# A four-layer graph network on one core: a third output bank in the last layer, one bank for transposed h, and a new order on every engine

## The chip, the core and the metric

The kernel runs on one core of a Trainium2 chip. The core has five engines with a queue of instructions each, which wait for one another by semaphores: TensorE (PE in the profile; its weight loads are PEld) multiplies matrices and writes to PSUM, VectorE (DVE), ScalarE (ACT) and GpSimd (POOL) work element by element, and SyncE (SP) issues the transfers. PSUM has 8 banks of 512 float32 numbers in each of 128 partitions. The metric is the device time of one launch in microseconds. The median before the change was 299.49 us.

## The reference

32 independent graphs of 256 nodes with 128 features pass through four residual layers. Each begins with a layer norm and a ReLU:

```python
def _layernorm(x, axis=-1, eps=1e-05):
    m = jnp.mean(x, axis=axis, keepdims=True)
    v = jnp.var(x, axis=axis, keepdims=True)
    return (x - m) / jnp.sqrt(v + eps)
h = jnp.maximum(_layernorm(x, axis=-1), 0.0)
x = x + _L0_gnn_ref(h, adj, L0_gnn_W, L0_gnn_a)
h = jnp.maximum(_layernorm(x, axis=-1), 0.0)
x = x + _L1_gnn_ref(h, adj, L1_gnn_a0, L1_gnn_a1, L1_gnn_a2, L1_gnn_a3)
h = jnp.maximum(_layernorm(x, axis=-1), 0.0)
x = x + _L2_gnn_ref(h, L2_gnn_adj, adj, L2_gnn_weight, L2_gnn_bias)
h = jnp.maximum(_layernorm(x, axis=-1), 0.0)
x = x + _L3_gnn_ref(h, adj, L3_gnn_W, L3_gnn_a)
```

Layers 0 and 3 are graph attention: Wh = h W, scores s1 of the row plus s2 of the column with W h and the vector a, leaky ReLU, softmax over the edges, times Wh. Layer 3 has an ELU behind that. Layer 1 scores an edge by the product of h of its two nodes, weighted by a vector for the relation, and averages h itself. Layer 2 sums h over the edges of each relation and multiplies by the relation's matrix.

## The kernel before

A unit is one layer of one graph: n counts 128 of them. The order (ORDER) is layer 0 of graphs 0 to 15, layer 1 of the same, layer 2, layer 3, and then the same for graphs 16 to 31. So units 0 to 15 and 64 to 79 are layer 0, 16 to 31 layer 1, 32 to 47 layer 2, 48 to 63 layer 3, and 112 to 127 layer 3 of the second half.

Every engine runs its own `pipeline` over a table of entries (stage, lag, layers). In step s it goes through the table from top to bottom and issues the stage for unit s - lag, if that unit's layer is meant. So a lag sets in which step a stage comes, and the place in the table its order within the step. At a border between layers a step holds stages of both. The tables are written out by hand; nothing is reordered later.

The way of a unit of layer 0 or 3: VectorE takes statistics (`statistics`, L574), aggregates them to mean and variance (`mean_and_variance`, L582) and adds eps (`add_eps`, L588). GpSimd raises to the power -0.5 (`inverse_deviation`, L346), subtracts the mean (L354) and scales (L360). TensorE transposes h (`put_hT`, L823) and ScalarE copies it with a ReLU to hT (`take_hT`, L447). TensorE multiplies by the weights (`put_v`, L851). ScalarE takes exponentials of the scores (L471) and scales the values (L479). TensorE transposes the row scores (`put_z`, L888), VectorE combines them with the edges (`take_rows`, L644, writes pT), and TensorE makes the output (`put_o`, L926 and L929). VectorE inverts the sums (L654, L656). In layer 0 it then adds the residual (L670). In layer 3 ScalarE takes the ELU's two parts (`elu_parts`, L516 and L517, written expy and relu_y), and VectorE adds them (`elu`, L678) and adds x (`add_x`, L687, writes result). In layer 0 ScalarE also masks the edges (L456), TensorE transposes them (`put_edgesT`, L838) and ScalarE copies them (L466). In layer 1 VectorE rectifies h (`rectify`, L593); in layer 2 it multiplies minus the mean by the deviation (`minus_mean`, L598), and ScalarE normalizes (L437).

Banks before: transposed h uses bank 0 in layer 0, where bank 1 holds the transposed edges, and banks 0 and 1 in turn in layers 1 and 3. Outputs use banks 6 and 7 in turn, so an output waits until the one two units earlier has been taken. The weights of layers 0 and 3 (w_gat, a_gat) are both loaded on ScalarE's queue and prepared in banks 6 and 7 ahead of the first unit.

## Time and profile before

| | us |
|---|---|
| three runs | 299.09, 299.49, 300.00 |
| the profiled execution | 299.55 |
| its span | 297.7 |
| TensorE busy | 279.9 (94%) |
| VectorE busy | 261.3 (88%) |
| ScalarE busy | 260.2 (87%) |
| GpSimd busy | 224.8 (76%) |

The span is what the records of the profile cover; the execution's own time is 1.85 us longer. Busy shares are averages over four layers that load the engines differently, and matmuls overlap, so that a busy TensorE may still be slower than its own pace. So the distance between the starts of one recurring instruction says more. Idle time in brackets is that of the engine before the row, with what ended it.

### The profile page before, as it was taken

How to read it: one execution, taken by the hardware profiler on the slowest of the kernel's cores; microseconds unless marked ns; L12 is line 12 of the kernel's file. 1: busy time of each engine (PE TensorE's matmuls, PEld its weight loads, DVE VectorE, ACT ScalarE, POOL GpSimd, SP SyncE). 2: the span in 40 equal slices, each digit the busy share in tenths (PEclk: the TensorE clock that was granted, in tenths of full speed). 3: DMA queues.
4: the chain of work that ended last, by engine and by line, in shares of the span. 5: the costliest groups of instructions: out<-in, count | busy, mean ns of one | idle time of the engine just before them, and what ended most of it. 6: DMA issues, size and time to landing. Idle time of an engine off the chain costs nothing.

```text
span 297.7 us, 8186 instructions
## 1 busy us (share of the span) xinstructions
PE 279.9 (94%) x2250; PEld 259.4 (87%) x2250; DVE 261.3 (88%) x1355; ACT 260.2 (87%) x849; POOL 224.8 (76%) x363
## 2 busy tenths in 40 slices
PE   1899999999998999999999999999999899999992
PEld 1799998888987999998888999998888799999991
DVE  2689999888888898999999999988888889799995
ACT  3799997799999985899999889799999998589993
POOL 4987777676776999987768787777677699997800
PEclk9999999999999999999999999999999999999997
DMA  6925555310000000011111660000000000001223
GB/s 185 356 72 160 166 166 148 116 47 0 2 1 2 0 3 1 3 36 55 53 57 53 191 204 1 3 1 2 0 3 0 3 1 0 2 3 36 74 72 107
DMA packets 15949, 17.77 MB, mean 60 GB/s; under 512 B 2720, under 2 KB 11808, under 8 KB 15904
## 3 DMA queue, kind: packets, MB, share of 16 engines
q1 hardware_dynamic: 15072, 17.11, 18.2%
q8 instruction: 19, 0.31, 0.5%
q10 hardware_dynamic: 832, 0.13, 0.3%
q14 instruction: 26, 0.21, 0.3%
HBM read 13.05 MB, written 4.19 MB: 58 GB/s over the span
## 4 chain that ended last, share of the span: by engine, by line
PE 67%; DVE 20%; ACT 6%; issue 3%; DMA 1%; ACTq 0%; DVEq 0%
PE bank L929 19%; PE bank L875 9%; PE bank L880 9%; DVE pT L644 6%; PE bank L851 6%; PE bank L823 5%; PE bank L914 5%; PE bank L900 4%; DVE result L687 4%; DVE st L574 3%; PE bank L926 3%; PE bank L888 2%; PE bank L882 2%; PE bank L838 2%; DVE expy L678 2%
## 5 line engine op out<-in xcount | busy, mean ns | idle before, releaser
L346 POOL TENSOR_TENSOR rs<-ve,minus_half 128x2 f32<-128x2 f32 x128 | 89.9, 702 | 53.7 <-DVE ve L588 51.9
L929 PE MATMUL bank<-val,pT 128*128 128x129 f32 x512 | 74.7, 275 | 0.0
L929 PEld LDWEIGHTS bank<-val,pT 128*128 128x128 f32 x512 | 67.9, 193 | 0.0
L360 POOL TENSOR_TENSOR h<-h,rs 128x256 f32<-128x256 f32 x96 | 59.8, 623 | 0.1
L644 DVE SCALAR_TENSOR_TENSOR pT<-bank,val,edgesT 128x256 f32<-128x256 f32 x128 | 55.8, 478 | 3.7 <-PE bank L888 3.4
L574 DVE BATCH_NORM_STATS2 st<-x 128x6 f32<-128x128 f32 x192 | 44.3, 272 | 0.0
L851 PE MATMUL bank<-w_gat,hT 128*128 128x131 f32 x256 | 42.2, 288 | 0.3 <-ACT hT L447 0.2
L354 POOL TENSOR_TENSOR h<-x,mv 128x256 f32<-128x256 f32 x64 | 39.9, 623 | 2.5
L479 ACT ACTIVATE val<-bank,val 128x128 f32<-128x128 f32 x128 | 41.3, 391 | 0.0
L926 PE MATMUL bank<-ident,vsum 128*128 128x128 f32 x128 | 35.5, 278 | 3.3 <-DVE x L670 1.0
L823 PE MATMUL bank<-ident,h 128*128 128x128 f32 x192 | 38.5, 283 | 0.0
L880 PE MATMUL bank<-hT,haT 128*128 128x256 f32 x128 | 37.5, 388 | 0.1
L625 DVE CUSTOM_DVE_ANT_0 neg_s<-bank,upper 128x256 f32<-128x256 f32 x64 | 24.7, 422 | 13.3 <-ACT upper L497 13.1
L929 PEld LDWEIGHTS bank<-h,pT 128*128 128x128 f32 x256 | 31.1, 191 | 5.8 <-issue 2.0
L851 PEld LDWEIGHTS bank<-w_gat,hT 128*128 128x128 f32 x256 | 34.5, 195 | 1.5 <-issue 1.1
L929 PE MATMUL bank<-h,pT 128*128 128x129 f32 x256 | 34.1, 276 | 1.6 <-ACT pT L509 1.6
L875 PE MATMUL bank<-edgesT,h 128*128 128x256 f32 x128 | 32.6, 380 | 0.0
L582 DVE BATCH_NORM_AGGREGATE mv<-st 128x2 f32<-128x6 f32 x256 | 30.4, 160 | 0.4
L447 ACT ACTIVATE hT<-bank 128x256 f32<-128x256 f32 x64 | 26.2, 409 | 4.6 <-PE bank L823 4.2
L502 ACT ACTIVATE prob<-neg_s,neg_max 128x256 f32<-128x256 f32 x64 | 28.7, 497 | 0.0
L437 ACT ACTIVATE h<-x,nb,rs 128x128 f32<-128x128 f32 x64 | 27.8, 483 | 0.0
L588 DVE TENSOR_SCALAR ve<-mv 128x2 f32<-128x2 f32 x128 | 27.4, 214 | 0.0
(80 smaller groups left out, 664.8 us busy)
## 6 DMA issues: line engine op xcount, KB each, us to landing
edges<-in_adj SPq DMA_DIRECT2D x32, 256.0 KB, 3.5
xin<-in_x SPq DMA_DIRECT2D x32, 128.0 KB, 2.7
out_x<-result SPq DMA_DIRECT2D x32, 128.0 KB, 1.7
w_rel<-in_L_gnn_weight SPq DMA_DIRECT2D x1, 256.0 KB, 3.5
w_gat<-in_L_gnn_W ACTq DMA_DIRECT2D x2, 64.0 KB, 3.4
a_rel<-in_L_gnn_a SPq DMA_DIRECT2D x4, 0.5 KB, 4.3
bias<-in_L_gnn_bias SPq DMA_DIRECT2D x1, 64.0 KB, 3.6
a_gat<-in_L_gnn_a ACTq DMA_DIRECT2D x2, 1.0 KB, 3.5
```

The lines of the kernel that those rows point to most:

```text
L346: pool.tensor_tensor(rs[:, g % WIDE], ve[:, g % WIDE], minus_half[:, :], ALU.pow).then_inc(rs_ready, 1)
L354: pool.tensor_tensor(h[:, n % HS, :, 0:D], xin[:, g % XS] if layer == 0 else x1[:, g % WIDE], mv[:, g % WIDE, :, 0:1].to_broadcast([P, T, ...
L360: pool.tensor_tensor(h[:, n % HS, :, 0:D], h[:, n % HS, :, 0:D], rs[:, g % WIDE, :].rearrange("p (t o) -> p t o", o=1).to_broadcast([P, T, ...
L479: last = act.activation(val[:, k, t, 0:D], bank_v(n)[:, t, 0:D], ACT.Copy, scale=val[:, k, t, D:D + 1])
L574: last = dve.bn_stats(st[:, g % WIDE, t], src[:, t])
L644: last = dve.scalar_tensor_tensor(pT[:, n % 4, u], bank_z(n)[:, 0], val[:, k, u, D + 2:D + 3], edgesT[:, g % WIDE, u], ALU.max, ALU.mult)
L823: last = pe.transpose(bank_x(n)[:, t * P:(t + 1) * P], h[:, n % HS, t, 0:D], ident[:, :])
L851: last = pe.matmul(bank_v(n)[:, t], hT[:, n % 4, t * P:(t + 1) * P], w_gat[layer // 3][:, 0:D + 3], start=True, stop=True)
L875: last = pe.matmul(z[:, 0], h[:, n % HS, u, 0:D], edgesT[:, g % WIDE, u], start=(u == 0), stop=(u == T - 1))
L880: pe.matmul(z[:, t], haT[:, n % 4, t * P:(t + 1) * P], hT[:, n % 4], start=True, stop=False, skip_group_check=True)
L926: pe.matmul(bank_o(n)[:, t, 0:D], vsum[:, k:k + 1].to_broadcast([P, P]), ident[:, :], start=True, stop=False, is_transpose=True, skip_grou ...
L929: last = pe.matmul(bank_o(n)[:, t], pT[:, n % 4, u, t * P:(t + 1) * P], values[:, u], start=(u == 0 and layer == 1), stop=(u == T - 1), sk ...
```

## The change

Six things are changed.

- Outputs have a third bank, bank 1, in layer 3, from unit 48 to 57 and from 112 to 127 (the least recently used of three); from unit 58 to 63 and in the other layers they have two. Where a third bank is in use an output waits for the one three units earlier. The transposed edges, which need bank 1 in layer 0, wait for the last such output.
- Transposed h has bank 0 alone. So `put_hT` of a unit waits for `take_hT` of the unit before.
- Eps comes into the variance by the aggregation: the statistics have three more numbers a row, (0, 0, D * EPS), written once, and `bn_aggr` reads nine numbers in place of six. `add_eps` and its tile ve are gone; the power on GpSimd takes the variance from mv.
- The last layer's weights are loaded by SyncE behind x of graph 2 and prepared in units 4, 6 and 7 of layer 0, in columns of bank 0 that transposed h leaves free.
- `elu_parts` waits for `add_x` of four units before, which is the tile that it overwrites.
- All tables of lags are new, in lags and in order.

The lags that matter here, before and after: TensorE v 4 to 5, edges 4 to 5, z 5 to 6 (layer 1: 4 to 5), pT 6 to 7, o 7 to 8, transposed h stays at 3. ScalarE `take_hT` 5 to 4, `mask_edges` 4 to 5, `take_edgesT` 5 to 6, `elu_parts` 9 to 10, `scale_hT` 6 to 4, `exponentials` 7 to 6, `take_mh` 8 to 6, `normalize` 5 to 4. VectorE `take_rows` 8 to 9, `invert_sums` 10 to 11, `elu` 12 to 13, `add_x` 14 to 13, `rectify` 5 to 4, `minus_mean` 5 to 3. GpSimd 8 and 9 to 14, 15 and 16 throughout, with the power now last in a step. SyncE 8 to 11.

```diff
-LAG_MAX = 14
-SP_LAG = 8
+LAG_MAX = 16
+SP_LAG = 11
-def banks_of_hT():
...
-HT_BANK, HT_AFTER, EDGEST_AFTER = banks_of_hT()
+def banks_of_o():
+    least_used, last, bank, after = [6, 7, 1], {}, {}, {}
+    for n, (layer, _) in enumerate(ORDER):
+        third = layer == 3 and (n + 6 >= len(ORDER) or ORDER[n + 6][0] == 3)
+        bank[n] = next(b for b in least_used if b != 1 or third)
+        after[n] = last.get(bank[n])
+        last[bank[n]] = n
+        least_used.remove(bank[n])
+        least_used.append(bank[n])
+    return bank, after
+O_BANK, O_AFTER = banks_of_o()
+THIRD = [n for n in range(len(ORDER)) if O_BANK[n] == 1]
-        st = sb("st", [P, WIDE, T, 6])
+        st = sb("st", [P, WIDE, T, 9])
-        ve = sb("ve", [P, WIDE, T])
         def bank_x(n):
-            return bank[HT_BANK[n]][:, 0:N]
+            return bank[0][:, 0:N]
         def bank_o(n):
-            return bank[6 + n % 2][:, 0:T * (1 + D)].rearrange("p (t c) -> p t c", t=T)
+            return bank[O_BANK[n]][:, 0:T * (1 + D)].rearrange("p (t c) -> p t c", t=T)
...
@@ sync: loads of the first units
+                if k == 2:
+                    sp.dma_start(w_gat[1][:, 0:D], w3).then_inc(gat_loaded[1], 16)
+                    sp.dma_start(a_gat[1][:, :], a3.rearrange("(c p) o -> p (c o)", c=2), allow_slow_non_contiguous=True).then_inc(gat_loaded[1], 16)
@@ gpsimd
-            pool.wait_ge(ident_ready, 7)
+            pool.memset(st[:, :, :, 6:8], 0.0).then_inc(ident_ready, 1)
+            pool.memset(st[:, :, :, 8:9], D * EPS).then_inc(ident_ready, 1)
+            pool.wait_ge(ident_ready, 9)
-                pool.wait_ge(ve_ready, nth(ALL, n))
-                pool.tensor_tensor(rs[:, g % WIDE], ve[:, g % WIDE], minus_half[:, :], ALU.pow).then_inc(rs_ready, 1)
+                pool.wait_ge(mv_ready, nth(ALL, n))
+                pool.tensor_tensor(rs[:, g % WIDE], mv[:, g % WIDE, :, 1], minus_half[:, :], ALU.pow).then_inc(rs_ready, 1)
...
@@ scalar, take_hT: the last layer's weights in units 4, 6 and 7
+                if ORDER[n] == (0, 4):
+                    scale_a(1)
+                    take_wT(1, bank[0])
+                if ORDER[n] == (0, 6):
+                    take_wa(1, bank[0])
+                if ORDER[n] == (0, 7):
+                    act.wait_ge(norms_put, 1)
+                    act.activation(norm_sums[:, :], bank[0][0:1, 500:504], ACT.Copy).then_inc(norms_taken, 1)
@@ scalar, elu_parts
                 act.wait_ge(rinv_ready, nth(ATTEND, n))
+                if nth(LAST, n) > 4:
+                    act.wait_ge(result_ready, nth(LAST, n) - 4)
@@ vector
-                    last = dve.bn_stats(st[:, g % WIDE, t], src[:, t])
+                    last = dve.bn_stats(st[:, g % WIDE, t, 0:6], src[:, t])
...
-            def add_eps(n, layer, g):
-                k = g % SLOTS
-                dve.wait_ge(mv_ready, nth(ALL, n))
-                dve.tensor_scalar(ve[:, g % WIDE], mv[:, g % WIDE, :, 1], EPS, None, ALU.add).then_inc(ve_ready, 1)
@@ vector, its table of lags: two of the entries
-                      (residual, 11, RGCN_REL), (take_rows, 8, LAST), (rectify, 5, MULTI_REL),
+                      (take_rows, 9, LAST), (mean_and_variance, 2, FIRST), (rectify, 4, MULTI_REL),
@@ tensor, put_hT
-                if HT_AFTER[n]:
...
+                if n > 0:
+                    pe.wait_ge(hT_ready, nth(ATTEND, n) - 1)
...
+                if ORDER[n] == (0, 4):
+                    put_wT(1, bank[0])
+                if ORDER[n] == (0, 6):
+                    put_wa(1, bank[0])
+                if ORDER[n] == (0, 7):
+                    pe.wait_ge(norms_ready, 2)
+                    pe.matmul(bank[0][0:1, 500:504], ones[:, :], norms[:, :], start=True,
+                              stop=True).then_inc(norms_put, 1)
@@ tensor, put_edgesT
+                if nth(FIRST, n) > 1:
+                    pe.wait_ge(edgesT_ready, nth(FIRST, n) - 1)
+                before = [m for m in THIRD if m < n]
+                if before and g % WIDE == 0:
+                    pe.wait_ge(y_ready, nth(LAST, before[-1]))
@@ tensor, put_o
-                if n >= 2:
-                    if ORDER[n - 2][0] == 3:
-                        pe.wait_ge(y_ready, nth(LAST, n - 2))
+                before = O_AFTER[n]
+                if before is not None:
+                    if ORDER[before][0] == 3:
+                        pe.wait_ge(y_ready, nth(LAST, before))
                     else:
-                        pe.wait_ge(o_taken, nth(NOT_LAST, n - 2))
+                        pe.wait_ge(o_taken, nth(NOT_LAST, before))
+                if n in THIRD:
+                    pe.wait_ge(edgesT_ready, nth(FIRST, n))
```

On TensorE, the start of the program before (ident,w_gat and a_four,w_gatT are the weights' preparation, ident,h transposed h, ident_bf,absent the edges, w_gat,hT v, ident,val the row transposes z):

```order
L800 MATMUL bank<-ident,w_gat 128x128 x2
L804 MATMUL bank<-a_four,w_gatT 128x4 x2
L808 MATMUL bank<-norms,ones 1x4
L823 MATMUL bank<-ident,h 128x128 x2
L838 MATMUL bank<-ident_bf,absent 128x128 x4
L851 MATMUL bank<-w_gat,hT 128x131 x2
L823 MATMUL bank<-ident,h 128x128 x2
L888 MATMUL bank<-ident,val 128x128 x2
L838 MATMUL bank<-ident_bf,absent 128x128 x4
L851 MATMUL bank<-w_gat,hT 128x131 x2
L854 MATMUL bank<-hsum,w_gat 128x2
L823 MATMUL bank<-ident,h 128x128 x2
```

and now:

```order
L816 MATMUL bank<-ident,w_gat 128x128
L821 MATMUL bank<-a_four,w_gatT 128x4
L835 MATMUL bank<-ident,h 128x128 x4
L877 MATMUL bank<-w_gat,hT 128x131 x2
L861 MATMUL bank<-ident_bf,absent 128x128 x4
L835 MATMUL bank<-ident,h 128x128 x2
L914 MATMUL bank<-ident,val 128x128 x2
L877 MATMUL bank<-w_gat,hT 128x131 x2
L880 MATMUL bank<-hsum,w_gat 128x2
L861 MATMUL bank<-ident_bf,absent 128x128 x4
L835 MATMUL bank<-ident,h 128x128 x2
L914 MATMUL bank<-ident,val 128x128 x2
```

The weights of the last layer and their norms are gone from the front, two units' h are transposed ahead of the first v, and each v stands one unit further behind its h.

On VectorE, one step of the overlap of layer 3 with the next half's layer 0, before:

```order
L582 BN_AGGR mv<-st 128x2 x2
L574 BN_STATS st<-xin 128x6 x2
L644 SCALAR_TENSOR_TENSOR pT<-bank,val,edgesT 128x256 x2
L687 SCALAR_TENSOR_TENSOR result<-expy,x 128x256
L654 TENSOR_SCALAR sums<-bank 128x2
L656 RECIPROCAL rinv<-sums 128x2
L588 TENSOR_SCALAR ve<-mv 128x2
L678 SCALAR_TENSOR_TENSOR expy<-expy,relu_y 128x256
```

and now:

```order
L606 BN_AGGR mv<-st 128x2 x2
L595 BN_STATS st<-xin 128x6 x2
L705 SCALAR_TENSOR_TENSOR result<-expy,x 128x256
L696 SCALAR_TENSOR_TENSOR expy<-expy,relu_y 128x256
L672 TENSOR_SCALAR sums<-bank 128x2
L674 RECIPROCAL rinv<-sums 128x2
L662 SCALAR_TENSOR_TENSOR pT<-bank,val,edgesT 128x256 x2
```

The eps addition is gone, and add_x (result) and the ELU sum (expy) stand next to each other behind the statistics, where add_x stood behind the rows (pT) before.

On VectorE in layer 2, before:

```order
L664 TENSOR_TENSOR x<-bank,xb 128x256
L588 TENSOR_SCALAR ve<-mv 128x2
L598 SCALAR_TENSOR_TENSOR nb<-mv,rs 128x2
L582 BN_AGGR mv<-st 128x2 x2
L574 BN_STATS st<-x 128x6 x2
```

and now:

```order
L682 TENSOR_TENSOR x<-bank,xb 128x256
L595 BN_STATS st<-x 128x6 x2
L606 BN_AGGR mv<-st 128x2 x2
L617 SCALAR_TENSOR_TENSOR nb<-mv,rs 128x2
L682 TENSOR_TENSOR x<-bank,xb 128x256
```

The product with minus the mean (nb) belongs to the unit just before that of the aggregation ahead of it, where it was three units before.

## Rows read from the trace of the kernel before

**Rows 1.** Busy time in stretches: length, then PE, PEld, DVE, ACT, POOL busy

```profile
48.00:92.00 44.00, 42.87 (x318) 37.34 (x316) 37.04 (x224) 40.93 (x95) 31.28 (x49) 1.00 0.14 40
92.00:114.00 22.00, 21.47 (x135) 19.72 (x136) 20.09 (x120) 18.38 (x48) 19.64 (x30) 1.00 0.01 2
137.00:171.00 34.00, 31.74 (x284) 29.30 (x283) 33.55 (x152) 32.46 (x126) 25.63 (x40) 1.00 0.27 85
188.00:233.00 45.00, 44.75 (x338) 39.49 (x336) 38.23 (x227) 42.83 (x102) 32.81 (x52) 1.00 0.01 2
233.00:255.00 22.00, 21.44 (x135) 19.69 (x136) 20.01 (x120) 18.41 (x48) 19.71 (x30) 1.00 0.01 2
```

**Rows 2.** Timeline of the first microseconds: start, duration, engine, line, operation [idle before]

```profile
6.73 0.15 DVE L588 TENSOR_SCALAR ve<-mv 128x2 f32<-128x2 f32 x1
6.96 0.70 POOL L346 TENSOR_TENSOR rs<-ve,minus_half 128x2 f32<-128x2 f32 x1 [0.91 <-DVE ve L588]
8.64 0.69 PE L823 MATMUL bank<-ident,h 128*128 128x128 f32 x2
8.76 0.69 POOL L346 TENSOR_TENSOR rs<-ve,minus_half 128x2 f32<-128x2 f32 x1
...
12.31 1.18 PE L851 MATMUL bank<-w_gat,hT 128*128 128x131 f32 x4
15.64 0.27 PE L926 MATMUL bank<-ident,vsum 128*128 128x128 f32 x1
16.75 0.38 PE L888 MATMUL bank<-ident,val 128*128 128x128 f32 x2
17.19 0.67 PE L851 MATMUL bank<-w_gat,hT 128*128 128x131 f32 x4
```

**Rows 3.** Timeline of TensorE: row transposes (L888) of units 15, 52, 58 and 71

```profile
47.51 0.38 PE L888 MATMUL bank<-ident,val 128*128 128x128 f32 x2
...
124.51 0.38 PE L888 MATMUL bank<-ident,val 128*128 128x128 f32 x2
...
137.10 0.38 PE L888 MATMUL bank<-ident,val 128*128 128x128 f32 x2
...
170.91 0.38 PE L888 MATMUL bank<-ident,val 128*128 128x128 f32 x2
```

**Rows 4.** Chain of waits, 140 to 150 us: start, length, piece

```profile
142.30 0.78 DVE pT L644 x2
...
143.93 0.15 DVE ve L588
...
144.93 0.78 DVE pT L644 x2
```

**Rows 5.** Timeline of VectorE and GpSimd around 129 and 143 us

```profile
129.26 0.41 DVE L687 SCALAR_TENSOR_TENSOR result<-expy,x 128x256 f32<-128x256 f32 x1
...
129.82 0.69 POOL L346 TENSOR_TENSOR rs<-ve,minus_half 128x2 f32<-128x2 f32 x1 [0.53 <-DVE ve L588]
129.92 0.40 DVE L678 SCALAR_TENSOR_TENSOR expy<-expy,relu_y 128x256 f32<-128x256 f32 x1
...
142.85 0.61 POOL L354 TENSOR_TENSOR h<-xin,mv 128x256 f32<-128x256 f32 x1
142.99 0.76 DVE L687 SCALAR_TENSOR_TENSOR result<-expy,x 128x256 f32<-128x256 f32 x1
```

**Rows 6.** Timeline of ScalarE: first ELU activation of two units in a row

```profile
152.30 0.42 ACT L516 ACTIVATE expy<-bank,rinv 128x128 f32<-128x128 f32 x1
...
155.30 0.51 ACT L516 ACTIVATE expy<-bank,rinv 128x128 f32<-128x128 f32 x1
```

**Rows 7.** Page, groups of instructions: the aggregation, count, busy, mean ns | idle before

```profile
L582 DVE BATCH_NORM_AGGREGATE mv<-st 128x2 f32<-128x6 f32 x256 | 30.4, 160 | 0.4
```

**Rows 8.** Timeline of the tail

```profile
290.78 0.37 ACT L516 ACTIVATE expy<-bank,rinv 128x128 f32<-128x128 f32 x1 [0.43 <-DVE rinv L656]
...
292.16 0.37 ACT L516 ACTIVATE expy<-bank,rinv 128x128 f32<-128x128 f32 x1 [0.23 <-DVE rinv L656]
```

More of the change, by code:

```diff
@@ L423, in _, with take_wT, take_wa @@
                 act.activation(a_four[i][:, 3:4], a_gat[i][:, 1:2], ACT.Copy, scale=SLOPE).then_inc(a_scaled, 1)
+            def take_wT(i, b):
                 act.wait_ge(wT_done, i + 1)
-                act.activation(w_gatT[i][:, :], ps_w[i][:, 0:D], ACT.Copy).then_inc(wT_ready, 1)
-            for i in range(2):
+                act.activation(w_gatT[i][:, :], b[:, 256:256 + D], ACT.Copy).then_inc(wT_ready, 1)
+            def take_wa(i, b):
                 act.wait_ge(wa_done, i + 1)
-                act.activation(w_gat[i][:, D:D + 4], ps_w[i][:, 256:260], ACT.Copy).then_inc(constants, 1)
-            for i in range(2):
-                last = act.activation(norms[:, 2 * i:2 * i + 2], ps_w[i][:, 256:258], ACT.Square)
-            last.then_inc(norms_ready, 1)
+                act.activation(w_gat[i][:, D:D + 4], b[:, 500:504], ACT.Copy).then_inc(constants, 1)
+                act.activation(norms[:, 2 * i:2 * i + 2], b[:, 500:502], ACT.Square).then_inc(norms_ready, 1)
+            scale_a(0)
+            take_wT(0, ps_w)
+            take_wa(0, ps_w)
             def normalize(n, layer, g):
@@ L795, in turn, with put_wT, put_wa @@
                 pe.wait_ge(g_step, g * G + AT[name])
[L797 to L798 removed]
+            pe.wait_ge(ident_ready, 9)
+            def put_wT(i, b):
                 pe.wait_ge(gat_loaded[i], GAT_WEIGHTS)
[L800 to L801 removed]
+                pe.transpose(b[:, 256:256 + D], w_gat[i][:, 0:D], ident[:, :]).then_inc(wT_done, 1)
+            def put_wa(i, b):
                 pe.wait_ge(wT_ready, i + 1)
                 pe.wait_ge(a_scaled, i + 1)
[L804 to L808 removed]
+                pe.matmul(b[:, 500:504], w_gatT[i][:, :], a_four[i][:, :], start=True, stop=True).then_inc(wa_done, 1)
+            put_wT(0, ps_w)
+            put_wa(0, ps_w)
             def put_hT(n, layer, g):
                 k = g % SLOTS
[L812 to L817 removed]
+                if n > 0:
+                    pe.wait_ge(hT_ready, nth(ATTEND, n) - 1)
                 if layer == 1:
```

99 lines of the change are left out of this document (35 added, 64 removed).

## The prediction

> **What bounds the kernel now.** I read the busy table by stretches first, then the starts of one recurring TensorE instruction, then the chain of waits where those starts spread out, and last the timeline around each spread.
>
> The stretches [rows 1] show TensorE (PE) nearly always busy, so the question is only where its steady pace is broken. It idles 1.13 us in 48 to 92 (layer 1), 0.53 in 92 to 114 (layer 2), and 0.25 and 0.56 in the second half's counterparts: 2.5 us together. In 137 to 171, where the last layer of the first sixteen units overlaps the first layer of the next sixteen, it idles 2.26, and there VectorE (DVE) is busy 33.55 of 34 us and ScalarE 32.46.
>
> Busy time hides stretched work, so I take the row transposes of line 888, one pair for each unit of layers 0 and 3 [rows 3]. Unit 2 comes at 16.75 [rows 2] and unit 15 at 47.51: 2.37 us a unit in layer 0, TensorE's own pace. Units 52 to 58 take 12.59, 2.10 a unit in the last layer, again its own pace. Units 58 to 71 take 33.81. At the two own paces, five units at 2.10 and eight at 2.37, they would take 29.4. So 4.4 us are lost there, the largest loss of the kernel.
>
> The chain of waits says on whom: between 142.30 and 144.93 it lies wholly on VectorE, 2.63 us for one unit [rows 4], of which 0.15 is the addition of eps (ve). From 152.30 to 155.30 ScalarE needs 3.00 us for a unit [rows 6], because a unit there carries ELU parts and also masking and edge copies. So first VectorE bounds, then ScalarE.
>
> **The change part by part.** The profiled execution took 299.55 us, a span of 297.7 and 1.85 around it; that is 0.06 above the median of 299.49, so a sum against the one serves for the other.
>
> *Start.* GpSimd (POOL) waits 0.91 us for unit 1's eps addition [rows 2], which stands behind the statistics of unit 2, which wait for a load. Now the power takes the variance directly and stands behind no later unit. With the 0.15 of the addition itself and a handover, GpSimd's chain starts about 1.2 us sooner, and the first transposes of h move from 8.64 to about 7.4; the last layer's weights no longer stand ahead of them either. From there GpSimd gives a unit each 1.80 (6.96 to 8.76). The new order needs h of unit 4 in place of unit 3 before the first full step: 7.4 + 4 x 1.80 = 14.6, then one output (15.64 to 16.75, 1.1 us), and unit 2's row transposes would come at 15.7. But the weight matmuls at 12.31 take 1.18 us against 0.67 for the same four at 17.19: by that spacing TensorE ran at the lower of its two levels (1.2 GHz) there, though the records grant it 1.00, and it had been little busy before. A sparser start keeps that cost, some 0.4. So 16.1 against 16.75, and one h transpose more is done (0.2), against 0.3 for the last layer's weight matmuls that now stand inside busy steps. Term: -0.5. Bounds: -1.3 if the level rises as soon as before, +0.5 if it rises two microseconds later. The two loads moved to SP's queue stand in front of x of unit 3 and later; those are needed 1.8 us apart and the bytes ahead of them are the same, so nothing.
>
> *VectorE in the overlap.* One unit loses the 0.15 of the eps addition. The last addition shows 0.41 at 129.26 and 0.76 at 142.99, where GpSimd's subtraction (142.85, 0.61) runs beside it [rows 5]. In the new order it stands right behind the statistics, when GpSimd has just been given its power; an ELU sum of the same shape is not stretched beside a power (129.92, 0.40, beside 129.82, 0.69). So the 0.35 should mostly go too: 2.63 - 0.15 - 0.35 = 2.13, next to TensorE's 2.10. What is then late is ScalarE: four units at 3.00 against 2.37 are 2.5 us, which no reordering removes. I take a loss of 2.5 in place of 4.4: -1.9. Bounds: -4.4 (all of it, if the longer pipeline covers ScalarE's burst) and +1.0 (the additions still collide and the ELU sum as well, and TensorE waits on ScalarE's ELU with less slack, since there the outputs have two banks again).
>
> The Trainium skill ("SBUF — State Buffer", Who interferes with whom) says that a VectorE instruction with two SBUF inputs is blocked by any GpSimd instruction that reads SBUF. The rows at 142.85 agree, those at 129.82 do not: the power reads SBUF as well and the ELU sum kept its 0.40. By that rule the addition would be blocked in the new place too, up to 0.70 a unit, and this gain would be lost; that is the first rival's case.
>
> *Borders of the layers.* Every consumer now stands one step further behind its producer (hT to v two steps, z two before o), so a late ScalarE or VectorE step reaches TensorE less often. Of the 2.5 us of idle time I take 0.7: the same work still has to pass ScalarE, 40.93 of 44 busy in layer 1. Term -0.7, bounds -2.5 and +0.5.
>
> *One bank for transposed h.* A transpose now waits for the copy of the unit before. Between them lies all the rest of a unit's work on TensorE, 2.10 us less the transposes, and the copy is one ScalarE instruction. Cost 0; if ScalarE is a whole step late it costs what ScalarE is late, which is in the bounds above.
>
> *Third output bank.* It lets an output start before the ELU parts of two units earlier are done. In the tail ScalarE waits 0.43 and 0.23 for the sums of the last two outputs [rows 8], which themselves waited for ScalarE to free a bank. With those outputs earlier, ScalarE runs through: 0.66. The last additions are also queued one step less behind (13 in place of 14), 0.25. Term -0.9, bounds -1.5 and +1.0 (two units' ELU parts, eight instructions of at most 0.37 us, are left later than before, partly beside TensorE).
>
> *Longer aggregation.* Nine numbers in place of six in 256 instructions of 160 ns [rows 7]. No row shows the longer form; it costs nothing, or half as much again, 80 ns twice a unit over some twelve bound units, 1.9. I take 0: the eps addition of two numbers took 0.15 too, so the time is hardly that of the numbers.
>
> Sum: -0.5 - 1.9 - 0.7 - 0.9 = -4.0. So 299.55 - 4.0, about 295.5 us.
>
> **The rivals.**
>
> First: the overlap stays as it is but for the 0.15. The additions collide with GpSimd at their new place, so VectorE keeps about 2.5 a unit over the seven to eight units it bounds: 1.1 in place of 1.9. ScalarE's bursts fall on outputs with two banks, so the border gain is nothing, and the start is a wash. For it: the same stretch shows both collision and none. Then -1.1 - 0.9 = -2.0: 297.5 us.
>
> Second, slower: VectorE and GpSimd in a tight circle. Rectifying (layer 1) moves from lag 5 to 4 and the product with minus the mean (layer 2) from 5 to 3, one VectorE step behind the aggregation whose power they need. The circle in layer 1 is a power (0.70), a scaling (0.61), a rectifying and two aggregations (some 0.6 by [rows 7]) and handovers (0.08 each by 6.73 + 0.15 against 6.96, four of them), 2.2 us; layer 1 gives a unit 44/16 = 2.75 [rows 1]. It decides once GpSimd is still at another 0.61 when the aggregation lands: 2.8. A collision of 0.35 on top makes 3.15, 0.4 a unit over 16 of the 32 units: +6.5, and 295.5 + 6.5 = 302 us. Against it: GpSimd is busy only 31.28 of 44 there. In layer 2 it is busier (19.64 of 22), but its power and bias addition, 0.70 and about as much, still fit in 22/16 = 1.38.
>
> Third: the longer pipeline hides ScalarE's burst also, and the borders' idle time halves: -4.4 - 1.2 - 0.5 - 0.9 = -7.0, 292.5 us.
>
> **How the numbers follow.** Forecast 295.5, chance 0.56. First rival 297.5, 0.24. Second 302, 0.13. Third 292.5, 0.07. The range is 292.9 to 299.8: it holds the forecast's own spread and the first rival's, and leaves out most of the second and third. A measurement tells 0.3% (0.9 us) from no change, so faster means under 298.6. All of the third, nearly all of the forecast's and three quarters of the first rival's chance lie there: 0.78. Within 0.3%: 0.09. Slower: 0.13.
>
> **What would show it.** First transposes of h near 7.4 us and unit 2's row transposes near 16.1. In the overlap the last addition at 0.41 and VectorE's unit near 2.15; ScalarE the one that is waited for, near 3.0 a unit. Units 58 to 71 in about 32. In the tail no ScalarE wait for inverted sums. If layer 1 takes over 2.75 a unit, with VectorE waiting for GpSimd at the rectifying, the second rival is right; if the last addition still shows 0.76, the first. The forecast is wrong if the overlap is not shorter by more than 1 us, or if any layer's own pace has changed.

## The result, and the profile after

Measured in the same session, the kernel before takes 299.43 us (299.09 to 300.0, four runs) and the kernel after 294.75 us (294.44 to 295.32, four runs): a ratio of 0.9844, interval 0.9822 to 0.9866. The profiled execution's span went from 297.7 to 292.9 us, 4.8 less. The forecast of 295.5 was 0.75 too high, within its range, and the direction was right. The sum was right for partly wrong reasons, though, and the stretches show it.

Where the prediction used line 888, line 914 does the same work now: the row transposes of a unit of layers 0 and 3. The timeline of TensorE in the kernel after, units 2, 14, 48, 58, 71, 78, 112 and 127 (start, duration, engine, line, operation):

```profile
15.80 0.38 PE L914 MATMUL bank<-ident,val 128*128 128x128 f32 x2
...
43.87 0.38 PE L914 MATMUL bank<-ident,val 128*128 128x128 f32 x2
...
112.85 0.38 PE L914 MATMUL bank<-ident,val 128*128 128x128 f32 x2
...
134.69 0.38 PE L914 MATMUL bank<-ident,val 128*128 128x128 f32 x2
...
167.27 0.38 PE L914 MATMUL bank<-ident,val 128*128 128x128 f32 x2
...
183.28 0.38 PE L914 MATMUL bank<-ident,val 128*128 128x128 f32 x2
...
251.44 0.38 PE L914 MATMUL bank<-ident,val 128*128 128x128 f32 x2
...
284.35 0.38 PE L914 MATMUL bank<-ident,val 128*128 128x128 f32 x2
```

The kernel before has units 2, 58 and 71 in [rows 2] and [rows 3]; these are its units 14, 48, 78, 112 and 127:

```profile
45.11 0.38 PE L888 MATMUL bank<-ident,val 128*128 128x128 f32 x2
...
116.38 0.38 PE L888 MATMUL bank<-ident,val 128*128 128x128 f32 x2
...
187.36 0.38 PE L888 MATMUL bank<-ident,val 128*128 128x128 f32 x2
...
257.41 0.38 PE L888 MATMUL bank<-ident,val 128*128 128x128 f32 x2
...
288.47 0.38 PE L888 MATMUL bank<-ident,val 128*128 128x128 f32 x2
```

The differences of these starts divide the 4.8 us. A border is the change from one layer to the next.

| stretch | what runs there | before | after | change |
|---|---|---|---|---|
| 0 to unit 2 | start | 16.75 | 15.80 | -0.95 |
| 2 to 14 | layer 0 | 28.36 | 28.07 | -0.29 |
| 14 to 48 | border, layer 1, border, layer 2 | 71.27 | 68.98 | -2.29 |
| 48 to 58 | layer 3 alone | 20.72 | 21.84 | +1.12 |
| 58 to 71 | layer 3 beside the next layer 0 | 33.81 | 32.58 | -1.23 |
| 71 to 78 | layer 0 | 16.45 | 16.01 | -0.44 |
| 78 to 112 | border, layer 1, border, layer 2 | 70.05 | 68.16 | -1.89 |
| 112 to 127 | layer 3 alone | 31.06 | 32.91 | +1.85 |
| 127 to the end | tail | 9.23 | 8.55 | -0.68 |

So the stretches with layers 1 and 2 gave most (-4.2), and the steps in which layer 3 runs alone lost 3.0, which the forecast doesn't have.

*The start.* Its timeline, GpSimd and TensorE:

```profile
5.63 0.69 POOL L351 TENSOR_TENSOR rs<-mv,minus_half 128x2 f32<-128x2 f32 x1
...
6.96 0.69 PE L835 MATMUL bank<-ident,h 128*128 128x128 f32 x2 [1.54 <-POOL h L365]
...
9.29 1.08 PE L877 MATMUL bank<-w_gat,hT 128*128 128x131 f32 x4
...
13.60 0.61 PE L877 MATMUL bank<-w_gat,hT 128*128 128x131 f32 x4
```

Unit 1's power (5.63) has no wait in brackets now, where [rows 2] had 0.91, and the first transposes of h come at 6.96 in place of 8.64. The weight matmuls still take 1.08 at 9.29 and only 0.61 at 13.60: the slow spacing at the start stayed, as reckoned. Before, GpSimd had finished unit 0's h at 8.23 (7.62 and 0.61 of scaling), and TensorE was still at the last layer's weights: the matmul of their norms ran at 8.52, 0.12 ahead of the transposes. So the later weights were needed for the transposes to move, as well as the shorter way to the power (experiment 11).

*A border.* Where layer 1 ends, TensorE transposes the last probabilities (prob), which ScalarE copies as pT for the outputs. Before, TensorE waited there for such a copy:

```profile
91.15 0.60 PE L900 MATMUL bank<-ident,prob 128*128 128x128 f32 x4
92.53 1.13 PE L929 MATMUL bank<-h,pT 128*128 128x129 f32 x8 [0.78 <-ACT pT L509]
93.50 0.60 PE L900 MATMUL bank<-ident,prob 128*128 128x128 f32 x4
```

and after:

```profile
86.34 0.60 PE L926 MATMUL bank<-ident,prob 128*128 128x128 f32 x4
...
87.67 0.60 PE L926 MATMUL bank<-ident,prob 128*128 128x128 f32 x4
...
89.00 1.03 PE L901 MATMUL bank<-edgesT,h 128*128 128x256 f32 x4
89.87 0.60 PE L926 MATMUL bank<-ident,prob 128*128 128x128 f32 x4
```

No wait is left, and layer 2's first gather (89.00, line 901) already runs between the last two transposes. From the fourth transposes before the last to the last it takes 8.36 us (81.51 to 89.87) against 10.15 (83.35 to 93.50), while a unit inside layer 1 went only from 2.66 to 2.64. The two stretches don't hold quite the same work: the one before has the score matmuls of three units and one pair of transposes of h, the one after the scores of two units and that gather. By what these rows take elsewhere in the same traces (1.1 and 0.22 us, against 0.87) this is 0.4 us of the difference, so the border itself gave some 1.3. Of the 10.15 us the busy table has TensorE idle in 0.81; the rest of the 1.3 is counted as busy. Most of both lies at one place: from 91.15 to 92.53 TensorE takes 1.38 us where the same row is followed after 0.44 elsewhere. The second half shows the same place at 232.19 to 233.56.

*Layer 3 beside layer 0.* VectorE and GpSimd in the kernel after:

```profile
138.57 0.69 POOL L351 TENSOR_TENSOR rs<-mv,minus_half 128x2 f32<-128x2 f32 x1 [0.30 <-DVE mv L606]
138.77 0.41 DVE L705 SCALAR_TENSOR_TENSOR result<-expy,x 128x256 f32<-128x256 f32 x1
139.10 0.42 DVE L696 SCALAR_TENSOR_TENSOR expy<-expy,relu_y 128x256 f32<-128x256 f32 x1
139.23 0.76 POOL L365 TENSOR_TENSOR h<-h,rs 128x256 f32<-128x256 f32 x1
```

The last addition (result) takes 0.41 beside the power, as forecast, and the ELU sum 0.42. GpSimd's scaling, which starts 0.13 behind the ELU sum, takes 0.76 in place of 0.61: here the one that starts second is the longer one. For the addition [rows 5] had 0.76 beside a subtraction that had started before it. Successive additions here come 2.29 apart (136.48, 138.77, 141.06). ScalarE is what follows, with the first ELU activation of two units 3.00 apart, as in [rows 6]:

```profile
149.38 0.50 ACT L537 ACTIVATE expy<-bank,rinv 128x128 f32<-128x128 f32 x1
...
152.38 0.60 ACT L537 ACTIVATE expy<-bank,rinv 128x128 f32<-128x128 f32 x1
```

*Layer 3 alone.* Here the same two instructions do the opposite:

```profile
127.10 0.61 POOL L365 TENSOR_TENSOR h<-h,rs 128x256 f32<-128x256 f32 x1
127.55 1.01 DVE L705 SCALAR_TENSOR_TENSOR result<-expy,x 128x256 f32<-128x256 f32 x1
127.67 0.61 POOL L359 TENSOR_TENSOR h<-x,mv 128x256 f32<-128x256 f32 x1
128.24 0.87 POOL L351 TENSOR_TENSOR rs<-mv,minus_half 128x2 f32<-128x2 f32 x1
128.49 0.82 DVE L696 SCALAR_TENSOR_TENSOR expy<-expy,relu_y 128x256 f32<-128x256 f32 x1
...
271.82 1.39 DVE L705 SCALAR_TENSOR_TENSOR result<-expy,x 128x256 f32<-128x256 f32 x1
272.31 0.61 POOL L359 TENSOR_TENSOR h<-x,mv 128x256 f32<-128x256 f32 x1
```

Before, result took 0.41 in this place [rows 5]. Now it lies over GpSimd's scaling (127.10) and subtraction (127.67) and takes 1.01, and 1.39 in the second half; the ELU sum takes 0.82 where it took 0.40. It starts beside the power (128.24 to 129.11) and ends 0.23 behind the start of the next scaling (129.08). Units 56 to 58 are 2.15, 3.29 and 2.38 apart, against 2.00, 2.18 and 2.07 before. The first additions of layer 3 come seven units behind its first row transposes (lags 13 and 6), so units 49 to 55 don't show it. The reason is in VectorE's table of steps: add_x stands last in it and the ELU sum near its head. Where layer 0 runs beside layer 3, its statistics fill the place ahead of add_x and GpSimd is at its power by then. Where layer 3 is alone, add_x comes right behind take_rows (pT), when GpSimd is in the middle of scaling and subtracting.

The page's row of the aggregation, to set beside [rows 7], and ScalarE's only wait left in the tail, beside [rows 8]:

```profile
L606 DVE BATCH_NORM_AGGREGATE mv<-st 128x2 f32<-128x9 f32 x256 | 32.7, 169 | 5.1
```

```profile
286.71 0.37 ACT L537 ACTIVATE expy<-bank,rinv 128x128 f32<-128x128 f32 x1 [0.43 <-DVE rinv L674]
```

### The profile page after: what moved, and what is told of

It reads as the page before. It is cut to its first block, busy times and chain, and to the rows that moved or that the text cites. A ratio compares the mean times of both kernels' runs of the same rounds, so it can differ in the third digit from the quotient of the medians.

```text
span 292.9 us, 8092 instructions
## 1 busy us (share of the span) xinstructions
PE 274.8 (94%) x2250; PEld 256.8 (88%) x2250; DVE 259.3 (89%) x1227; ACT 258.2 (88%) x850; POOL 224.5 (77%) x365
## 4 chain that ended last, share of the span: by engine, by line
PE 71%; DVE 17%; ACT 4%; issue 4%; POOL 1%; DVEq 0%; POOLq 0%
PE bank L959 20%; PE bank L901 9%; PE bank L906 9%; PE bank L877 6%; PE bank L835 5%; DVE pT L662 5%; PE bank L944 5%; PE bank L926 5%; DVE expy L696 4%; DVE result L705 4%; PE bank L956 3%; PE bank L914 3%; PE bank L861 2%; PE bank L908 2%; DVE st L595 2%
## 5 line engine op out<-in xcount | busy, mean ns | idle before, releaser
L351 POOL TENSOR_TENSOR rs<-mv,minus_half 128x2 f32<-128x2 f32 x128 | 89.5, 700 | 47.9 <-DVE mv L606 47.5
L365 POOL TENSOR_TENSOR h<-h,rs 128x256 f32<-128x256 f32 x96 | 61.1, 637 | 0.1
L498 ACT ACTIVATE val<-bank,val 128x128 f32<-128x128 f32 x128 | 42.9, 417 | 0.0
L877 PE MATMUL bank<-w_gat,hT 128*128 128x131 f32 x256 | 40.1, 280 | 0.0
L606 DVE BATCH_NORM_AGGREGATE mv<-st 128x2 f32<-128x9 f32 x256 | 32.7, 169 | 5.1
L906 PE MATMUL bank<-hT,haT 128*128 128x256 f32 x128 | 36.5, 380 | 0.0
L521 ACT ACTIVATE prob<-neg_s,neg_max 128x256 f32<-128x256 f32 x64 | 29.3, 516 | 2.1 <-DVE neg_max L646 2.0
L466 ACT ACTIVATE hT<-bank 128x256 f32<-128x256 f32 x64 | 27.2, 425 | 4.4 <-PE bank L835 3.9
L537 ACT ACTIVATE expy<-bank,rinv 128x128 f32<-128x128 f32 x64 | 25.4, 401 | 5.7 <-DVE rinv L674 5.4
L835 PEld LDWEIGHTS bank<-ident,h 128*128 128x128 f32 x192 | 23.6, 151 | 6.4 <-POOL h L365 1.6
```

Source lines behind the costliest of these rows:

```text
L351: pool.tensor_tensor(rs[:, g % WIDE], mv[:, g % WIDE, :, 1], minus_half[:, :], ALU.pow).then_inc(rs_ready, 1)
L365: pool.tensor_tensor(h[:, n % HS, :, 0:D], h[:, n % HS, :, 0:D], rs[:, g % WIDE, :].rearrange("p (t o) -> p t o", o=1).to_broadcast([P, T, ...
L498: last = act.activation(val[:, k, t, 0:D], bank_v(n)[:, t, 0:D], ACT.Copy, scale=val[:, k, t, D:D + 1])
L835: last = pe.transpose(bank_x(n)[:, t * P:(t + 1) * P], h[:, n % HS, t, 0:D], ident[:, :])
L877: last = pe.matmul(bank_v(n)[:, t], hT[:, n % 4, t * P:(t + 1) * P], w_gat[layer // 3][:, 0:D + 3], start=True, stop=True)
L906: pe.matmul(z[:, t], haT[:, n % 4, t * P:(t + 1) * P], hT[:, n % 4], start=True, stop=False, skip_group_check=True)
```

## The experiments

Twelve more kernels were timed, each against the kernel before (299.7 to 299.8 us in these sessions). Times are medians; ratios are to the kernel before with their 95% intervals. My theory after the result: the gain comes from TensorE's and ScalarE's steps at the borders, and the new place of VectorE's ELU additions saves time in the overlap and costs time in layer 3 alone. The rivals: depth of the pipeline alone, the removed eps addition, or the third bank.

**1. The new structure with the old tables.** One bank for hT, folded eps, late weights and the third bank, but the tables of all engines, SyncE's lag too, as before.

```diff
-            pipeline([(put_z, 6, RGCN_REL), (put_o, 8, FIRST), (put_z, 5, MULTI_REL), (put_o, 8, LAST),
...
+            pipeline([(put_o, 7, LAST), (put_o, 7, FIRST), (put_o, 7, MULTI_REL), (put_z, 5, FIRST),
...
```

> The changed kernel's banks, folded eps and late weights, but with the old tables of lags and order on all five engines (eps addition left out of VectorE's). My theory: most of the gain is the tables' depth and order. Eps alone saves 0.15 us on some 8 to 16 bound units, the freed start about 0.5, the third bank a little in the tail: 297.0 to 298.5 us. Rival: the gain is the banks' and eps's, and the tables only tidy up: 294.5 to 295.5. If one bank for transposed h hurts with the shallow pipeline (the copy then stands between two transposes), it may be above 299.

Measured: 301.37 us, 1.0048 (1.0030 to 1.0066). With the old tables the rest of the change makes the kernel 1.7 us slower, so there is no gain without the new tables; they bring 6.6 us from here. That isn't theirs alone: with them the fold (experiment 6) and the third bank (experiments 2 and 4) are needed.

**2. Two output banks.** The third bank taken out of the kernel after.

```diff
-        third = layer == 3 and (n + 6 >= len(ORDER) or ORDER[n + 6][0] == 3)
+        third = False
```

> The changed kernel with two output banks throughout. My theory: in layer 3 VectorE is the bound (2.25 to 3.3 us a unit), so that the third bank is worth little: 294.8 to 295.8 us, with the loss in the last ten units. Rival: the third bank carries the last layer, since an output otherwise waits for ScalarE's ELU parts of two units before with next to no slack: 296.5 us or more.

Measured: 295.85 us, 0.9870 (0.9852 to 0.9887); its interval overlaps that of the kernel after. The bank is worth about 1 us here by the medians, and by the intervals anything from nothing to 2. The profiled execution is the fastest of five (294.26, the others 295.73 to 296.02), so its trace doesn't show all of the loss. The spacing tells more: steps of layer 3 alone go 2.33 and 2.17 in place of 2.00 and 2.17, but units 56 to 58 go 2.33, 2.23, 2.34, without the 3.29. The likely reason is that the slower steps leave room for the stretched additions; this was not tested by itself.

**3. The additions behind the statistics of layer 3.** Tests the reading of layer 3 alone.

```diff
-            pipeline([(invert_sums, 11, FIRST), (mean_and_variance, 2, RGCN_REL), (elu, 13, LAST),
+            pipeline([(invert_sums, 11, FIRST), (mean_and_variance, 2, RGCN_REL), 
...
-                      (statistics, 1, RGCN_REL), (statistics, 1, LAST), (invert_sums, 11, MULTI_REL),
+                      (statistics, 1, RGCN_REL), (statistics, 1, LAST), (add_x, 14, LAST), (elu, 13, LAST), (invert_sums, 11, MULTI_REL),
...
-                      (mean_and_variance, 2, MULTI_REL), (statistics, 1, FIRST), (add_x, 13, LAST)])
+                      (mean_and_variance, 2, MULTI_REL), (statistics, 1, FIRST)])
```

> The changed kernel with VectorE's two ELU additions moved behind the statistics also in the steps that hold layer 3 alone (add_x lag 14 and elu lag 13, both right behind statistics of LAST; the overlapped steps keep their order). My theory: between units 48 and 58 and between 112 and 127 the changed kernel loses 1.1 and 1.9 us against the one before, because there result (1.01 us at worst) and the ELU sum (0.75) run beside GpSimd's scaling and subtraction; moved, they show 0.41 and 0.42, VectorE's unit falls from 2.75 to about 2.3, and the time to 291.5 to 293 us. Rival: the loss comes from ScalarE's or TensorE's order and the collisions only fill a wait: 294.3 to 295 us, with the wait elsewhere.

Measured: 291.45 us, 0.9730 (0.9711 to 0.9749), faster than both kernels of the case. Its VectorE and GpSimd in layer 3 alone:

```profile
128.34 0.43 DVE L705 SCALAR_TENSOR_TENSOR result<-expy,x 128x256 f32<-128x256 f32 x1
128.45 0.86 POOL L351 TENSOR_TENSOR rs<-mv,minus_half 128x2 f32<-128x2 f32 x1
128.69 0.41 DVE L696 SCALAR_TENSOR_TENSOR expy<-expy,relu_y 128x256 f32<-128x256 f32 x1
```

Both additions now lie beside the power and keep 0.43 and 0.41. Units 55 to 58 take 6.21 us against 7.82 in the kernel after (6.25 before), and 119 to 124 take 10.54 against 12.98 (10.46). That is 4.1 us, the price of the collisions; the overlap, 58 to 71, gives 0.55 of it back (33.13 against 32.58). The reading is shown.

**4. The same with two banks.** Is the third bank needed once the additions are out of the way?

```diff
-        third = layer == 3 and (n + 6 >= len(ORDER) or ORDER[n + 6][0] == 3)
+        third = False
```

(on the kernel of experiment 3)

> The changed kernel with VectorE's ELU additions behind the statistics (as in the run with that alone, 291.45 us) and two output banks in layer 3. My theory: with the collisions gone TensorE bounds layer 3, and two banks then make every output wait for the ELU parts of two units before; where collisions hid it the two-bank kernel took 2.32 and 2.18 us a unit against 2.00 and 2.17 with three. 0.16 over some 20 units: 293.5 to 295.5 us. Rival: the third bank is worth nothing here either: 291.3 to 292.3.

Measured: 295.95 us, 0.9871 (0.9848 to 0.9894). Here the bank is worth 4.5 us. TensorE waits for ScalarE's ELU to free a bank:

```profile
129.94 0.32 PE L956 MATMUL bank<-ident,vsum 128*128 128x128 f32 x1 [0.85 <-ACT relu_y L538]
```

So the third bank and the place of the additions are each worth little where the other limits. The kernel before ran 2.00 and 2.18 with two banks, so it is the new tables that need the third.

**5. More slack between VectorE and GpSimd.** Rectifying and minus the mean moved back to lag 5, which undoes the second rival's mechanism.

```diff
-                      (minus_mean, 3, RGCN_REL), (take_z, 8, MULTI_REL), (residual, 11, RGCN_REL),
+                      (minus_mean, 5, RGCN_REL), (take_z, 8, MULTI_REL), (residual, 11, RGCN_REL),
...
-                      (take_rows, 9, LAST), (mean_and_variance, 2, FIRST), (rectify, 4, MULTI_REL),
+                      (take_rows, 9, LAST), (mean_and_variance, 2, FIRST), (rectify, 5, MULTI_REL),
```

> The changed kernel with rectify at lag 5 and minus_mean at lag 5 again, so that VectorE no longer stands one step behind the power it needs. My theory: the circle VectorE, GpSimd, VectorE does not bind in layers 1 and 2: within 0.4 us of the changed kernel, 294.4 to 295.1. Rival (the second one of the prediction): it costs something already, and this is 1 us or more faster.

Measured: 304.15 us, 1.0142 (1.0124 to 1.0160). Layer 1 takes 2.95 us a unit in place of 2.64. The timeline of one step:

```profile
68.22 0.29 DVE L612 TENSOR_SCALAR h<-h 128x256 f32<-128x256 f32 x1
...
68.58 0.60 ACT L516 ACTIVATE upper<-bank 128x512 f32<-128x512 f32 x1 [0.19 <-PE bank L908]
...
68.66 0.41 PE L835 MATMUL bank<-ident,h 128*128 128x128 f32 x2
...
69.36 0.42 DVE L646 CUSTOM_DVE_ANT_0 neg_s<-bank,upper 128x256 f32<-128x256 f32 x1 [0.32 <-ACT upper L516]
```

ScalarE waits 0.19 for TensorE's scores, VectorE 0.32 for ScalarE's upper part, and the rectifying, behind both in VectorE's step, is followed 0.44 later by the transposes of h that need it. With the rectifying one step later the circle TensorE, ScalarE, VectorE, TensorE closes within one step. Layer 2 stays at 1.31 us a unit, so it is the rectifying's lag that costs, not that of minus the mean. The short lag which I had priced as a danger is what keeps layer 1 on TensorE's pace. The last four steps of layer 1 show 2.41, 2.42, 1.33 and 2.20 here as well: these two lags of VectorE don't make the gain at the border.

**6. The eps addition back in the new tables.**

```diff
-                pool.wait_ge(mv_ready, nth(ALL, n))
-                pool.tensor_tensor(rs[:, g % WIDE], mv[:, g % WIDE, :, 1], minus_half[:, :], ALU.pow).then_inc(rs_ready, 1)
+                pool.wait_ge(ve_ready, nth(ALL, n))
+                pool.tensor_tensor(rs[:, g % WIDE], ve[:, g % WIDE], minus_half[:, :], ALU.pow).then_inc(rs_ready, 1)
...
+                      (statistics, 1, RGCN_REL), (add_eps, 2, RGCN_REL), (statistics, 1, LAST), (add_eps, 2, LAST), (invert_sums, 11, MULTI_REL),
```

> The changed kernel with the eps addition back on VectorE (a step of its own for every unit, behind that unit's aggregation; six numbers aggregated again), all else as changed. My theory: it costs where VectorE bounds, some 25 units of layer 3 and the overlap at 0.15 to 0.3 us: 297 to 300 us. Rival: GpSimd's lateness does not matter and the 0.15 is hidden: within 1 us of the changed kernel, 294.5 to 295.7.

Measured: 317.84 us (314.83 to 318.49), 1.0557 (1.0516 to 1.0598). Layer 2 takes 2.28 us a unit in place of 1.31:

```profile
105.05 0.15 DVE L611 TENSOR_SCALAR ve<-mv 128x2 f32<-128x2 f32 x1
105.27 0.70 POOL L351 TENSOR_TENSOR rs<-ve,minus_half 128x2 f32<-128x2 f32 x1 [0.89 <-DVE ve L611]
105.94 0.72 POOL L374 TENSOR_TENSOR xb<-x,bias 128x256 f32<-128x256 f32 x1
106.01 0.67 DVE L621 SCALAR_TENSOR_TENSOR nb<-mv,rs 128x2 f32<-128x2 f32 x1 [0.49 <-POOL rs L351]
...
107.07 0.71 PE L948 MATMUL bank<-w_rel,mhT 128*128 128x128 f32 x4 [0.70 <-DVE x L686]
```

The power waits 0.89 for ve; the product with minus the mean (106.01) waits 0.49 for the power, and lies then beside GpSimd's bias addition, where it takes 0.67. In the kernel after it takes 0.29, beside only the end of that addition, and in the kernel before mostly 0.15. TensorE waits 0.70 behind all of it. This is the second rival's tight circle, in layer 2, and the folded eps is what keeps it open. The eps addition was tried at one place of the table only; another place may cost less.

**7. The fold alone, in the kernel before.**

```diff
-        st = sb("st", [P, WIDE, T, 6])
+        st = sb("st", [P, WIDE, T, 9])
...
-                      (add_eps, 3, LAST), (add_eps, 3, RGCN_REL), (minus_mean, 5, RGCN_REL),
+                      (minus_mean, 5, RGCN_REL),
```

> The kernel before with eps folded into the aggregation and nothing else (tables, banks and weights as before, the eps addition taken out of VectorE's table). My theory: 0.15 us off each unit that VectorE bounds (units 58 to 71) and less delay of GpSimd: 297.5 to 299 us, with the aggregation at 160 to 170 ns. Rival: the shortened VectorE step shifts the ELU additions against GpSimd and the gain is lost in collisions: 299 to 300.5.

Measured: 302.05 us, 1.0076 (1.0060 to 1.0092), 2.3 us slower although VectorE has 128 instructions fewer. In layer 3 alone:

```profile
133.51 0.61 POOL L360 TENSOR_TENSOR h<-h,rs 128x256 f32<-128x256 f32 x1
133.66 0.75 DVE L675 SCALAR_TENSOR_TENSOR expy<-expy,relu_y 128x256 f32<-128x256 f32 x1
134.08 0.79 POOL L354 TENSOR_TENSOR h<-x,mv 128x256 f32<-128x256 f32 x1
```

GpSimd no longer waits for ve, and its scaling and subtraction now meet the ELU sum, whose mean went from 414 to 568 ns. Units 56 to 58 come 2.78, 2.58 and 2.59 apart. In the trace layer 3 alone loses 3.4 us against the kernel before, in both halves together, of a span that is 4.1 longer; the profiled execution is the slowest of the six. This accounts for experiment 1: there the fold is in too, and shows the same spacing (2.05, 2.57, 2.60).

**8. One bank for hT alone, in the kernel before.**

```diff
-            bank[n], after[n] = turn % 2, last[turn % 2]
-            last[turn % 2] = ("hT", n)
-            turn += 1
+            bank[n], after[n] = 0, last[0]
+            last[0] = ("hT", n)
```

> The kernel before with transposed h in bank 0 in all layers, so that a transpose waits for the copy of the unit before (it did so in layer 0 already), nothing else. The old tables with the new banks took 301.37 us. My theory: this wait is what costs there: the old ScalarE table copies hT a step later, so in layers 1 and 3 the copy falls between two transposes: 300.5 to 302.5 us. Rival: it costs nothing, as the forecast said of the new tables: 299.3 to 300.1.

Measured: 299.45 us, 0.9990 (0.9979 to 1.0001). No cost; this expectation was wrong and the prediction's 0 right.

**9. Depth alone.** In the kernel before, everything behind hT one lag later, orders unchanged.

```diff
-            pipeline([(put_o, 7, LAST), (put_o, 7, FIRST), (put_o, 7, MULTI_REL), (put_z, 5, FIRST),
...
+            pipeline([(put_o, 8, LAST), (put_o, 8, FIRST), (put_o, 8, MULTI_REL), (put_z, 6, FIRST),
...
```

> The kernel before with one step more between transposed h and all that follows it (TensorE v, z, edges, pT and o each one lag later, ScalarE's and VectorE's stages behind them too), its order within a step, its banks and eps as before. Theory that depth alone gave the gain at the borders of the layers: 1.3 us at each border of layers 1 and 2 and about 1 at each of layers 0 and 1, less one more step at start and end: 295 to 297.5 us. Rival: the order within the steps gave it, and depth alone costs a step: 299.5 to 301.

Measured: 309.59 us, 1.0338 (1.0317 to 1.0359). This longer pipeline by itself costs 10 us. Its last four steps of layer 1 take 10.72 us, with the scores of three units like the 10.15 before: the border's gain isn't depth.

**10. One lag of ScalarE.** Normalizing of layer 2 at lag 6 in place of 4, to see whether layer 2 rests on it.

```diff
-                      (normalize, 4, RGCN_REL), (take_hT, 4, LAST), (scale_hT, 4, MULTI_REL),
+                      (normalize, 6, RGCN_REL), (take_hT, 4, LAST), (scale_hT, 4, MULTI_REL),
```

> The changed kernel with ScalarE's normalizing of layer 2 at lag 6 in place of 4, as late before TensorE's gathering product as in the kernel before. Theory: the gain of 1.3 us at each border of layers 1 and 2 comes from ScalarE normalizing earlier, ahead of layer 1's last exponentials: 296.5 to 298 us. Rival: it comes from the exponentials and copies standing earlier, not from this: 294.4 to 295.3.

Measured: 325.24 us, 1.0850 (1.0836 to 1.0865), a miss by 27 us. Layer 2 goes at 2.39 us a unit:

```profile
108.10 1.10 PE L901 MATMUL bank<-edgesT,h 128*128 128x256 f32 x4 [0.84 <-ACT mhT L503]
...
109.24 0.38 ACT L503 ACTIVATE mhT<-bank 128x256 f32<-128x256 f32 x1 [1.24 <-PE bank L901]
...
109.76 0.42 DVE L682 TENSOR_TENSOR x<-bank,xb 128x256 f32<-128x256 f32 x1 [1.08 <-PE bank L944]
```

TensorE's gather waits 0.84 for ScalarE's copy, the copy 1.24 for the gather: another closed circle. It says how narrow the lag is. On the border, for which it was meant, it says a little: the last four steps of layer 1 go 2.42, 2.41, 1.34 and 4.00, against 2.41, 2.42, 1.33 and 2.20 in the kernel after. The first three keep their length with the late normalizing, so the early one doesn't make them short.

**11. The last layer's weights in front**, as in the kernel before.

```diff
+            act.dma_start(w_gat[1][:, 0:D], w3).then_inc(gat_loaded[1], 16)
...
-                if ORDER[n] == (0, 4):
-
-                    put_wT(1, bank[0])
```

> The changed kernel with the last layer's weights loaded on ScalarE's queue and prepared ahead of the first unit, as before (in bank 7), all else as changed. My theory: the later weights were worth about half of the start's gain: the second weights' load lands near 6.6 us, first transposes of h at about 8.2 in place of 6.96, but TensorE has 0.3 us less in its full steps: 295 to 296 us. Rival: GpSimd sets the start and this costs nothing: 294.3 to 294.8.

Measured: 295.09 us, 0.9848 (0.9835 to 0.9861), not to be told from the kernel after. The first transposes of h come at 9.05 in place of 6.96, behind the weights again, with unit 0's h ready at 6.90 as in the kernel after. The x of unit 2 arrives at 6.97 in place of 5.97, so the place of the loads, which the prediction had at nothing, matters too. Still unit 2 is only 1.0 later and unit 127 only 0.5: most of a later start is made up before layer 0 is through.

**12. Masks of eight graphs earlier**, in layer 2 (on the kernel of experiment 3), to take ScalarE's burst out of the overlap.

```diff
+            def mask_early(n, layer, g):
+                if g < 16 and g % 2 == 1:
+                    mask_edges(UNIT[0, 16 + g // 2], 0, 16 + g // 2)
...
-                      (upper_part, 6, MULTI_REL), (take_hT, 4, MULTI_REL), (mask_edges, 5, FIRST),
+                      (upper_part, 6, MULTI_REL), (take_hT, 4, MULTI_REL), (mask_late, 5, FIRST),
```

(`mask_late` leaves graphs 16 to 23 out; `mask_early` stands in layer 2 at lag 6)

> The same with the ELU additions moved, three banks, and ScalarE masking the edges of graphs 16 to 23 already in layer 2 of the first half (one for every two units), where it is 17.5 of 22 us busy, in place of the overlap. Theory: in the overlap ScalarE's 3.0 us a unit are then the bound (units 64 to 68 at 2.6, 2.6, 3.1, 3.0); without the mask's 0.57 they fall to about 2.45, 2.0 to 2.5 us are saved: 289 to 290 us. Rival: VectorE (2.29 a unit, and residuals beside ELU) takes its place: 290.5 to 291.5.

Measured: 291.47 us, 0.9741 (0.9712 to 0.9769), the same as experiment 3. Between 145 and 160 us ScalarE is busy 12.76 us in place of 15.00, and VectorE 14.83 in both kernels. From 143 to 164 ScalarE now waits 1.5 us for VectorE's inverted sums, against 0.2 in experiment 3:

```profile
154.70 0.83 DVE L713 SCALAR_TENSOR_TENSOR result<-expy,x 128x256 f32<-128x256 f32 x1
155.45 0.41 DVE L704 SCALAR_TENSOR_TENSOR expy<-expy,relu_y 128x256 f32<-128x256 f32 x1
```

The last addition is at 0.83 again and the residual addition of layer 0 follows in the same step; units there still come up to 3.57 apart. TensorE's waits there still name ScalarE's ELU (1.13 us at 151.49), and with it the bank that the ELU must free, since outputs have two banks there. So two limits or three lie close together, and relieving one alone gives nothing.

## Why the prediction was right, and where it was not

*What bounds the kernel.* TensorE's pace and breaks in it: right. Even a unit's own pace moved, which the prediction had called a sign of error: 2.37 to 2.30 in layer 0. TensorE idles in neither; the mean of a weight matmul (w_gat, hT) fell from 288 to 280 ns.

*Start*, -0.5: measured -0.95. The wait of 0.91 went as forecast, the transposes came 0.44 earlier than I had them (6.96, not 7.4), and the slow spacing stayed. I had priced GpSimd's chain alone; TensorE's transposes at 8.64 had stood behind the last layer's weights, and experiment 11 holds them there with the eps addition gone. Unit 2 came anywhere from 15.70 to 16.37 in executions with this same start, so half a microsecond here can be chance. Layer 0's own pace gave another 0.7 that no term has (0.29 and 0.44 in the table).

*VectorE in the overlap*, -1.9: measured -1.23. The mechanism was right in each part: the last addition at 0.41, ScalarE next at 3.00 a unit. VectorE's unit came to 2.29 where I had 2.13. The addition lost its 0.35 (0.68 to the next start before, 0.33 now), but the eps addition had not filled 0.15 of a step: the ELU sum started 0.06 behind it (143.93 and 143.99), and the rows around take 0.06 more now. The sum of the overlap was 0.7 too good.

*Borders*, -0.7: measured -4.2 over both stretches from layer 0 to layer 3. This is the mis-sized term. I bounded it by the busy table's idle time, 2.5 us in all, and took a quarter. That bound was no bound: the end of layer 1 had lost some 1.3 us in each half, of which 0.8 was idle and the rest counted as busy, and layer 1's own pace gave another 0.3 in each half. The remaining microsecond is spread over single rows of 0.05 to 0.25 us. I should have priced the borders as I priced the overlap, by the spacing of a recurring instruction against its pace.

*Longer aggregation*, 0: 169 ns in place of 160, 2.3 us busy over the kernel and on no path that shows. *One bank for hT*, 0: shown by experiment 8 with the old tables.

*Third bank and tail*, -0.9: measured -0.68. Of ScalarE's two waits one stayed (0.43), one went. With two banks (experiment 2) the same stretch takes 8.99, so some 0.4 of it is the bank's. But the third bank does most of its work in layer 3 alone, which I hadn't counted: with it every other step of the new tables takes 2.00 there, without it 2.33.

*What I missed*: +3.0 where layer 3 runs alone. The prediction looked at the additions' new place only in the overlap, where statistics of layer 0 stand ahead of them. With layer 3 alone those rows are absent from the step and the neighbour is pT. The first rival named this collision but in the wrong stretch. It and the borders' excess (-3.5) nearly cancelled, and that is why 295.5 came so close: the closeness is luck.

The Trainium skill ("SBUF — State Buffer", Who interferes with whom) has a VectorE instruction with two SBUF inputs contend with any GpSimd instruction that reads SBUF. The runs agree for the scaling, the subtraction and the bias addition (result 0.41 to 1.01 and 1.39, nb 0.15 to 0.67) and disagree for the power: over the fourteen traces the 202 ELU sums and last additions that overlap with nothing on GpSimd but a power take 0.38 to 0.42, and the 191 that overlap only with its large instructions 0.74 in the median. Weighing rule and row was right; what it lacked was to ask in every stretch which of GpSimd's instructions is the neighbour.

*The second rival*, slower at 302: not in this kernel. Its circle of VectorE and GpSimd closes in experiment 6, at 318 us. Experiments 5 and 10 close others, over TensorE and ScalarE, at 304 and 325 us.

What stays open is which of TensorE's and ScalarE's lags makes the border shorter. It is not the banks and the fold (experiment 1: 10.14 for those four steps), not depth in the old order (9), not the two lags of VectorE (5) and, for three of the four steps, not the early normalizing (10); the tables were not divided further. Nor is it known what shortened a weight matmul from 288 to 280 ns.

## What to carry to other kernels

Price a border between stages by the spacing of one recurring instruction against its own pace, not by the idle time of the busy table, which counts stretched work as work. When a table gives an instruction a place, list its neighbours for every mix of stages that a step can hold: the same line was free in one mix and cost 3 us in another. Where engines hand work round in a circle, one lag or one small instruction more costs not its own duration but a step's worth in every unit, so take it out or put it in alone before judging it.
